# FFN setup moved into the first waits: gates, gated weights, w1/w2 split tables and their load signals in an attention + mixture-of-experts block on one core

## The reference

```python
h = layernorm(x) * (1 + ca) + sa
x = x + ga * attn(h)        # 16 heads of 8, causal window of 32 keys, softmax, output projection o_w, o_b
h = layernorm(x) * (1 + cb) + sb
x = x + gb * ffn(h)
# ffn: top-2 of 8 experts by h @ gate_w, softmax of the two scores = weights wE;
#   o_e = gelu(h @ w1_e + b1_e) @ w2_e + b2_e
#   out = sum_e wE_e * (layernorm(h + o_e) * ln_g_e + ln_b_e)
```

## Time and profile before

| what | value |
|---|---|
| runs shown | 306.83, 306.78, 305.35 us; median 306.78 us |
| profiled execution's own time | 306.58 us |
| its span, first to last instruction | 304.6 us |
| mean granted TensorE clock | 0.951 of full |
| busy share of the span | PE 89%, weight loads 73%, DVE 61%, ACT 52%, POOL 44% |
| SP's issue of the two small DMAs of b2_rows | 0.73 and 0.64 us |
| a store of 128 KB, issue to landing | 1.8 us |
| chain that ended last, by engine | PE 71%, DVE 14%, ACT 6%, POOL 4%, issue 3%, DMA 1% |

### The profile page before, as it was taken

The page is one execution under the profiler, slowest core; times in us unless marked ns, Lnnn a source line. Parts: engine busy times, 40 slices in busy tenths (PEclk is TensorE's granted clock), DMA queues, the critical chain, the costliest instruction groups (busy, mean ns, idle before and its releaser), DMA issues.

```text
span 304.6 us, 7790 instructions
## 1 busy us (share of the span) xinstructions
PE 271.8 (89%) x3069; PEld 222.7 (73%) x3069; DVE 185.7 (61%) x570; ACT 159.9 (52%) x419; POOL 134.6 (44%) x245
## 2 busy tenths in 40 slices
PE   7989329999999999999999999999999999998980
PEld 4666219787788778877978778877887798777860
DVE  2548951586666656676568656765765665546066
ACT  1244501854566465755495348546673657545650
POOL 5040760126850546334732556164605461347256
PEclk9998855999979999999999999999999999999996
DMA  7910000000000000000000000000000000000000
GB/s 208 366 44 2 1 1 2 0 2 3 2 1 19 1 2 2 17 3 2 3 17 2 2 2 17 0 8 0 2 17 2 2 2 18 3 2 0 19 0 17
DMA packets 5651, 6.22 MB, mean 20 GB/s; under 512 B 336, under 2 KB 5104, under 8 KB 5360
## 3 DMA queue, kind: packets, MB, share of 16 engines
q1 hardware_dynamic: 5616, 5.74, 5.8%
HBM read 4.68 MB, written 1.05 MB: 19 GB/s over the span
## 4 chain that ended last, share of the span: by engine, by line
PE 71%; DVE 14%; ACT 6%; POOL 4%; issue 3%; DMA 1%; POOLq 0%; ACTq 0%; DVEq 0%
PE z L988 14%; PE score L946 10%; PE turns L839 6%; PE probT_bank L958 4%; ACT hid L471 4%; PE turns L841 4%; PE turns L840 4%; PE z L1009 3%; PE misc L971 3%; DVE xn L556 3%; PE turns L899 2%; PE misc L1031 2%; POOL rstd L331 2%; PE z L1008 2%; PE z L1007 2%
## 5 line engine op out<-in xcount | busy, mean ns | idle before, releaser
L471 ACT ACTIVATE hid<-turns,pack_ffn 128x256 f32<-128x256 f32 x128 | 50.7, 473 | 45.2 <-PE turns L841 45.2
L988 PE MATMUL z<-w,hid 128*128 128x128 f32 x480 | 65.4, 284 | 0.0
L988 PEld LDWEIGHTS z<-w,hid 128*128 128x128 f32 x480 | 57.0, 191 | 7.9 <-issue 7.3
L314 POOL TENSOR_TENSOR ypart<-ypart 128x256 f32<-128x256 f32 (+1 forms) x60 | 36.0, 600 | 20.7 <-DVE ypart L644 17.7
L839 PE MATMUL turns<-h_hi,w_hi 128*128 128x256 f32 x128 | 40.9, 320 | 3.7 <-ACT hid L471 3.1
L300 POOL TENSOR_SCALAR zvar<-zss 128x4 f32<-128x4 f32 x32 | 8.6, 270 | 78.8 <-DVE zss L630 69.3
L644 DVE SCALAR_TENSOR_TENSOR ypart<-z,zcoef,ln_gG 128x128 f32<-128x128 f32 x120 | 33.5, 342 | 11.8 <-POOL zcoef L305 11.8
L840 PE MATMUL turns<-h_lo,w_hi 128*128 128x256 f32 x128 | 37.0, 289 | 0.0
L841 PE MATMUL turns<-h_hi,w_lo 128*128 128x256 f32 x128 | 37.0, 289 | 0.0
L301 POOL TENSOR_TENSOR zrstd<-zvar,mhalf 128x4 f32<-128x4 f32 x32 | 32.4, 1014 | 2.7
L946 PEld LDWEIGHTS score<-kT,q_st 32*128 32x128 f32 x512 | 33.2, 198 | 0.4
(11 more groups left out here) (138 smaller groups left out, 459.7 us busy)
## 6 DMA issues: line engine op xcount, KB each, us to landing
w<-in_w SPq DMA_DIRECT2D x2, 1024.0 KB
out_x<-yout SPq DMA_DIRECT2D x8, 128.0 KB, 1.8
x_tokens<-in_x SPq DMA_DIRECT2D x1, 896.0 KB, 7.4
ln_g<-in_ln_g SPq DMA_DIRECT2D x1, 512.0 KB
pack_mod<-in_pack_mod SPq DMA_DIRECT2D x1, 385.0 KB, 3.0
pack_proj<-in_pack_proj SPq DMA_DIRECT2D x1, 193.0 KB, 5.0
pack_att<-in_pack_att SPq DMA_DIRECT2D x1, 130.5 KB, 4.9
x_tokens<-in_x SPq DMA_DIRECT2D x1, 128.0 KB, 2.9
```

The lines of the kernel that those rows point to most:

```text
L314: cf.link(g.tensor_tensor(ypart[:, tt, at:at + n, :], ypart[:, tt, at:at + n, :], ypart[:, tt, at + n:at + 2 * n, :], ALU.add))
L471: last = a.activation(hid[:, e, c, :], U[(e + 1) % 2][:, c * STEP:(c + 1) * STEP], ACT.Gelu, bias=b1[:, e, c:c + 1])
L988: last = mm(z_bank(f, q)[:, e * D:(e + 1) * D], hid[:, ee, c, tt * P:(tt + 1) * P], w2[:, ee * CH + c, :], start=False, stop=e == HALF - 1 ...
```

## The change

The gates and the gated output projection are set in DVE's `front` (`set_gates` behind `set_gates_abs`, `gated_w_o` ahead of `mask_q(0)`, `gated_b_o` behind `sum_b_o`); `set_w2_mean` stands at the end of DVE's `front`, behind `shift(0, 1)`; `set_ffn_bias` stands behind `take_h2T(0)`. w1 and w2 get load signals of their own, and ACT's w1_hi waits for w1 alone, `set_w2_mean` for w2 alone. On POOL `low_w1(0)`, `low_w1(1)` and `set_w2` move into `front`, behind `rstd_front(0)` and so ahead of `rstd_front(1)`. `gated_ln(0)` and `gated_ln(1)` both stand behind `rstd_second(0)` and a wait for `h2_s`. The counts of zero matmuls in `front` go from 6, 2, 6 to 3, 2, 2, and the first of `body(0)` from 6 to 8.

```diff
--- before.py
+++ after.py
@@ -158,6 +158,7 @@
         loaded_x, loaded_mod, loaded_proj = sem("loaded_x"), sem("loaded_mod"), sem("loaded_proj")
         loaded_att, loaded_mask, loaded_bo = sem("loaded_att"), sem("loaded_mask"), sem("loaded_bo")
         loaded_ffn, loaded_f, loaded_rest = sem("loaded_ffn"), sem("loaded_f"), sem("loaded_rest")
+        loaded_w1, loaded_w2 = sem("loaded_w1"), sem("loaded_w2")
         b2_moved = sem("b2_moved")
         set_pool, set_act, set_pe = sem("set_pool"), sem("set_act"), sem("set_pe")
         set_vec, set_b2, set_att, silu_s = sem("set_vec"), sem("set_b2"), sem("set_att"), sem("silu_s")
@@ -220,7 +221,7 @@
                 ins.then_inc(self.s, 1)
                 self.eng.wait_ge(self.s, self.n)
 
-        F_LOADS = [(w1, "w1"), (w2, "w2"), (b2, "b2"), (ln_b, "ln_b")]
+        F_LOADS = [(b2, "b2"), (ln_b, "ln_b")]
         ALL_F = 16 * (len(F_LOADS) + 1)
         x_view = t["x"].rearrange("b (n p) d -> p (b n) d", p=P)
         out_view = out.rearrange("b (n p) d -> p (b n) d", p=P)
@@ -241,6 +242,8 @@
             sp.dma_start(X[:, TILES:, :], x_view[:, TILES:, :]).then_inc(loaded_rest, 16)
             sp.dma_start(b_o[:, :], t["b_o"].partition_broadcast(P)).then_inc(loaded_bo, 16)
             load_pack("ffn", loaded_ffn)
+            sp.dma_start(whole(w1), t["w1"]).then_inc(loaded_w1, 16)
+            sp.dma_start(whole(w2), t["w2"]).then_inc(loaded_w2, 16)
             for dst, name in F_LOADS:
                 sp.dma_start(whole(dst), t[name]).then_inc(loaded_f, 16)
             sp.dma_start(ln_g[:, :, :], t["ln_g"].rearrange("e d -> (e d)").partition_broadcast(P)
@@ -346,11 +349,15 @@
 
                 if b == 0:
                     pool.wait_ge(gates_s, 1)
+                    pool.wait_ge(loaded_f, ALL_F)
                 g.tensor_tensor(ln_gG[:, b, :, :], ln_g[:, :, :], bc(gates[:, b, 1, :], 1, EXPERTS), ALU.mult)
                 g.tensor_tensor(ln_bG[:, b, :], ln_b[:, :], gates[0:EXPERTS, b, 1, :], ALU.mult).then_inc(lng_s, 1)
 
             def front(n):
                 rstd_front(n)
+                low_w1(0)
+                low_w1(1)
+                set_w2()
 
             def body(i, att, ffn, nxt):
                 n, f = i + 1, i - 1
@@ -358,27 +365,23 @@
                     rstd_front(n)
                 if ffn:
                     coefficients(f, 0)
-                if i == 0:
-                    low_w1(0)
                 if ffn:
                     coefficients(f, 1)
                 if i == 0:
-                    set_w2()
                     add_b_o(0)
-                    low_w1(1)
                 if nxt:
                     add_b_o(n)
                 if ffn and att:
                     add_experts(f, 1)
                     add_experts(f, 0)
-                if i == 1:
-                    gated_ln(1)
                 if att:
                     rstd_second(i)
                 if ffn:
                     coefficients(f, 2)
                 if i == 0:
+                    pool.wait_ge(h2_s, 1)
                     gated_ln(0)
+                    gated_ln(1)
                 if ffn:
                     coefficients(f, 3)
                 if ffn and att:
@@ -480,7 +483,7 @@
                 act.wait_ge(loaded_ffn, 16)
                 a.activation(ones_r[:, :], ones[:, :], ACT.Copy)
                 a.activation(center_r[:, :], center[:, :], ACT.Copy)
-                act.wait_ge(loaded_f, ALL_F)
+                act.wait_ge(loaded_w1, 16)
                 a.activation(w1_hi[:, :, :, :], w1[:, :, :, :], ACT.Copy).then_inc(w1_hi_s, 1)
 
             def body(i, att, ffn, nxt):
@@ -740,10 +743,14 @@
                 v.scalar_tensor_tensor(gates[:, :, :, :].rearrange(flat), gate_sign[:, :, :, :].rearrange(flat),
                                        -1.0, gates[:, :, :, :].rearrange(flat), ALU.add, ALU.mult).then_inc(gates_s, 1)
 
-            def gated_out():
+            def gated_w_o():
 
                 dve.wait_ge(gates_s, 1)
                 v.tensor_tensor(w_oG[:, :, :], bc(w_o[:, :], 1, BATCH), gates[:, :, 0, :], ALU.mult)
+
+            def gated_b_o():
+
+                dve.wait_ge(bias_o_s, 1)
                 v.tensor_tensor(b_oG[:, :, :], bc(b_o[:, :], 1, BATCH), gates[:, :, 0, :], ALU.mult).then_inc(b_o_s, 1)
 
             def sum_b_o():
@@ -761,18 +768,23 @@
                 split(b2_high[:, :], b2_low[:, :], b2[:, :]).then_inc(set_b2, 1)
 
             def set_w2_mean():
+                dve.wait_ge(loaded_w2, 16)
                 pre.link(v.reduce_sum(w2_mean[:, :], w2[:, :, :], axis=AX))
                 v.tensor_scalar(w2_mean[:, :], w2_mean[:, :], 1.0 / D, None, ALU.mult).then_inc(w2_mean_s, 1)
 
             def front(n):
                 set_masks()
                 set_gates_abs()
+                set_gates()
                 dve.wait_ge(loaded_att, 16)
+                gated_w_o()
                 mask_q(n)
                 sum_b_o()
+                gated_b_o()
                 stats_front(n + 1)
                 shift(n, 0)
                 shift(n, 1)
+                set_w2_mean()
 
             def body(i, att, ffn, nxt):
                 n, f = i + 1, i - 1
@@ -786,16 +798,10 @@
                     weights_T(f)
                 if nxt:
                     normed_front(n)
-                if i == 0:
-                    set_gates()
                 if ffn and att:
                     add_ln_b(f)
                     scale(f, 0)
                     zsum(f, 1)
-                if i == 0:
-                    set_ffn_bias()
-                    set_w2_mean()
-                    gated_out()
                 if ffn and att:
                     scale(f, 1)
                 if nxt:
@@ -806,6 +812,8 @@
                     add_attn(i)
                     normed_second(i)
                     take_h2T(i)
+                if i == 0:
+                    set_ffn_bias()
                 if ffn and att:
                     scale(f, 2)
                 if att:
@@ -1047,21 +1055,21 @@
 
             def front(n):
                 turn_x(n)
-                keep_warm(6)
+                keep_warm(3)
                 proj_k(n)
                 proj_q(n)
                 pe.wait_ge(loaded_att, 16)
                 keep_warm(2)
                 proj_v(n)
                 bias_of_v()
-                keep_warm(6)
+                keep_warm(2)
                 pe.wait_ge(mask_s, 1)
                 scores(n, 0)
 
             def body(i, att, ffn, nxt):
                 n, f = i + 1, i - 1
                 if i == 0:
-                    keep_warm(6)
+                    keep_warm(8)
                 if ffn and att:
                     down(f, 0, 0)
                 if att:
```

## The result

The changed kernel takes 303.91 us (median of 16 runs, 301.26 to 305.77); the kernel before, timed beside it, 306.6 (16 runs, 303.04 to 306.99). The ratio is 0.992, 95% interval 0.9891 to 0.995. So it is faster, by 2.5 by the ratio; the forecast was 5.5. A ratio is taken from the runs within 1.5% of their kernel's fastest, so it isn't always the quotient of the medians. The profiled execution takes 302.68, span 300.8, 3.9 under the profiled execution of before.

The account below looks back on a forecast made before the run. The first 60 us were taken as bound by DVE setup and two instructions stretched beside POOL; 4.15 there plus 1.4 from step 1's slow stretch made 5.5 off 306.58, giving 301.1 us, range 297.3 to 306.0.

Parts of the forecast that it names:

- What bounds it: First 60 us: nine us of DVE setup ahead of step 1's queries; b_oG (3.75) and xn (2.78) stretched beside POOL.
- DVE's new places: DVE in step 0: gates and w_oG fit idle 2.48, w2's mean idle 2.65, b_oG takes 0.42; no cost.
- ACT and POOL: Step 0's setup: w1_hi starts at 15.3 rather than 18.70; POOL's low_w1 and centring w2 run to 25.8.
- What is queued behind: rstd_front(1) stands behind POOL's weights: step 1's xn waits, is held, ends at 28.2; its turn_x comes 1.5 later.
- PE between: PE idle some 4 until 28.2, then one stretch of 3.4 at 1.2 GHz; step 0's last values end at 36.1.
- The path to the first up: Step 0: 1.35 gained on values, 0.6 on the output projection, 2.2 on xn; sum 4.15.
- Step 1's slow stretch: Half-clock stretch at 83.80 in step 1's turn from scores to ups: likelier gone than not, 1.4 gained.
- Sum: Whole kernel: 4.15 + 1.4 = 5.5 from 306.58 gives 301.1 us; with the slow stretch again, 302.5.
- the held clock: Rival: clock holds through PE's wait in step 0, 299.5, or 296.9 with scores and ups at 2.4 GHz; chance 0.22.
- the clock down for the whole stage: Rival: clock stays down until step 0's values at 38.9; 0.8 gained, 305.8, or 304.4 without slow stretch; chance 0.18.

## Why the prediction was wrong

The direction was right, the size twice too large. Point by point:

- **What bounds it** held: nine us of DVE setup and two instructions held by POOL. b_oG 0.42 and xn of step 0 0.60, as said; the run without the wait for h2_s confirms it is POOL's tables that hold xn.
- **DVE's new places**: nearly. The gates used up the wait before step 0's queries, and since PE came earlier it waited 1.03 for them; the scores started at 14.40, close to the 14.3 of the sum (15.85 before, less 1.6).
- **ACT and POOL**: right to about a us, w1_hi at 14.28 (15.3), w2 done at 25.39 (25.8).
- **What is queued behind**: right. xn of step 1 waited for POOL's rstd, was held by add_b_o(0), and ended at 27.4 (28.2), and taking w2's centring out of that queue won 3.4 by the ratios.
- **PE between**: the one stretch of 3.4 at half clock came as taken (27.05 to 30.40). In the three other profiles with the same step 0 it was 6.8, 6.8 and 10.1. That is a quantity that varies from execution to execution, and one value was taken for it. The values of step 0 ended at 34.9, 34.9, 36.9 and 36.9 in the four, around the 36.1 of the forecast.
- **The path to the first up**: 4.15 forecast, 5.34 between the two first profiles. But over the four profiles with each kernel's step 0 unchanged (the kernels with an edit in the turn alone included), step 1's weights start at 61.02, 60.13, 59.98 and 59.52 before, mean 60.2, and at 55.68, 56.51, 57.77 and 57.38 after, mean 56.8. The forecast, 61.02 - 4.15 = 56.9, is that mean; only the execution it was taken from stood 0.9 above its own kind. So this term was 3.3.
- **Step 1's slow stretch: this step failed.** "Likelier gone than not: 1.4 gained" took one stretch for an accident of one execution. Of eight profiles of kernels with these turns unchanged, seven had one or two of them (before 1 and 1; changed 2 and 1; with edits in step 0 alone 2, 1 and 1), and the eighth, with the zero matmuls in step 0's waits, had none. The fall always came 22.5 to 22.9 after the first weights of its step, in the turn from scores to ups, but in step 1, in steps 1 and 2, or in step 6. The earlier start of step 1 in the changed kernel did not remove them. What decides which turn is slow stays open. With one zero matmul in each turn the profiles of both kernels have none, and it won 1.9 in the kernel before and 2.9 in the changed one, by the ratios; but with the zero matmuls in step 0's waits alone the one profile had none either. The term was 0, not 1.4, as far as these profiles show.
- **Sum**: 3.3 + 0 instead of 4.15 + 1.4 leaves 303.3 against the profiled 306.58; the medians differ by 2.7, and with the turns held in both by 2.9, or 3.5 by the ratios. The rest, about half a us, lies within the spread of step 0 over four profiles (59.52 to 61.02 before, 55.68 to 57.77 after). The 1.9 that the zero matmul wins in the kernel before (by its interval 1.1 to 2.8) fits one slow turn of 1.45, the 2.9 in the changed kernel rather two, of which its two profiles had two and one.
- **The rivals**: neither the held clock (values at 34.5) nor the clock down for the whole stage (38.9) came; in all four profiles it was down for a part of the stage, 3.4 to 10.1, and the values lay between. A small instruction of POOL holds DVE too: add_b_o(0), 0.72, started 0.06 ahead of xn of step 1 and held it, and a small one of DVE is held, a centring of b2 on eight partitions for 2.13. The Trainium skill (SBUF — State Buffer, Who interferes with whom) says that the order of issue and not the shape of an instruction decides who is held; these rows agree.

## What to carry to other kernels

When setup is moved into a wait, follow the queue of the engine that takes it: here rstd, two instructions of 1 us, stood behind 8.3 us of weights, and putting 3.6 of these behind the next work won more than the whole change. A stretch at half clock that a profile shows once can come back in another step or another execution: take several profiles before counting it as won. And where an engine waits anyway, work that keeps TensorE's clock up costs nothing there: fourteen zero matmuls in two waits of step 0 were worth 1.4% by the two ratios, in the profiles 1.4 us of it in step 0 and 3.0 in later turns, these for a reason that is open.

## What was not expected of the hardware

The granted clock fell to half after 3.35 us of PE work without a gap (windows of the kernel with the moved scores), in which scores on 32 rows stood for most of the time: here PE's busy share alone did not tell whether the clock stays. Two DVE instructions in a row can each be held by an instruction of POOL: two xn took 5.06 instead of 0.60, the first to the end of one ln_gG, the second to the end of the next, and the 0.44 instruction on eight partitions that POOL ran between these did not let the second through.
